# A mixture-of-experts layer computed slot by slot instead of with all experts for all rows

## The reference

```python
x = x + tanh(g_xattn[0]) * conv_attention(layernorm(x), ...)        # stage A
# stage B: 8 experts, 2 chosen for each row, and a shared expert
h = layernorm(x)
probs = softmax(h @ Wr)                     # [2048, 8]
weights, chosen = top_k(probs, 2)           # not renormalized
moe = sum over e of C[:, e] * ((silu(h @ Wg[e]) * (h @ Wu[e])) @ Wd[e])     # Wg, Wu: 256 x 176, Wd: 176 x 256
shared = sigmoid(h @ Wsg) * ((silu(h @ Sg) * (h @ Su)) @ Sd)                # 704 hidden columns
x = x + tanh(g_ffn[0]) * (moe + shared)
x = x + tanh(g_xattn[1]) * causal_attention(layernorm(x), ctx)      # stage C, 16 heads
x = x + tanh(g_ffn[1]) * lora_moe_ffn(layernorm(x))                 # stage D
```

## Time and profile before

| | us |
|---|---|
| runs before: median of 3 (lowest, highest) | 870.32 (870.18, 876.75) |
| the profiled execution | 869.0 |
| its span, first to last instruction | 867.3 |
| mean granted clock of TensorE | 0.96 of 2.4 GHz |

### The profile page before, as it was taken

The page is one execution under the profiler, slowest core; times in us unless marked ns, Lnnn a source line. Parts: engine busy times, 40 slices in busy tenths (PEclk is TensorE's granted clock), DMA queues, the critical chain, the costliest instruction groups (busy, mean ns, idle before and its releaser), DMA issues.

```text
span 867.3 us, 13423 instructions
## 1 busy us (share of the span) xinstructions
PE 781.8 (90%) x4612; PEld 634.5 (73%) x4627; DVE 566.6 (65%) x1022; ACT 314.5 (36%) x507; POOL 159.2 (18%) x211
## 2 busy tenths in 40 slices
PE   3887888799999999999997999976699999999994
PEld 2575766688888888888884555545588888888883
DVE  4877778454654574367546898983355876868764
ACT  2220211223423343342234878756143423324221
POOL 2977877300000000021100111111010000000000
PEclk9999999999999999999998999996599999999998
DMA  7221321000000000001001122200000000000000
GB/s 279 73 91 49 104 67 30 1 1 1 1 0 0 0 0 0 0 0 33 19 1 46 54 69 75 60 31 13 1 1 1 2 24 0 0 24 0 24 1 25
DMA packets 22134, 26.09 MB, mean 30 GB/s; under 512 B 5328, under 2 KB 17744, under 8 KB 21968
## 3 DMA queue, kind: packets, MB, share of 16 engines
q1 hardware_dynamic: 22096, 25.60, 9.3%
HBM read 23.22 MB, written 2.10 MB: 29 GB/s over the span
## 4 chain that ended last, share of the span: by engine, by line
PE 70%; DVE 15%; issue 6%; POOL 4%; ACT 2%; SPq 1%; DMA 1%; DVEq 0%; POOLq 0%; ACTq 0%
PE bank L1590 21%; PE bank L1457 19%; PE bank L1470 11%; PE bank L1522 3%; PE bank L1512 3%; POOL A L459 2%; DVE A L874 2%; PE bank L1532 1%; DVE small L1071 1%; PE bank L1599 1%; DVE A L863 1%; POOL R L450 1%; PE bank L1385 1%; PE bank L1504 1%; DVE A L1081 1%
## 5 line engine op out<-in xcount | busy, mean ns | idle before, releaser
L1590 PE MATMUL bank<-R 128*128 128x512 f32 (+3 forms) x1080 | 214.5, 359 | 11.2 <-DVE R L1235 4.9
L1590 PEld LDWEIGHTS bank<-R 128*128 128x128 f32 (+1 forms) x1080 | 181.0, 190 | 44.3 <-DVE R L1235 5.2
L1457 PE MATMUL bank<-R 128*128 128x512 f32 x768 | 186.2, 392 | 1.9 <-issue 1.9
L1457 PEld LDWEIGHTS bank<-R 128*128 128x128 f32 x768 | 140.3, 188 | 29.4 <-issue 2.1
L1019 DVE TENSOR_TENSOR A<-bank,A 128x512 f32<-128x512 f32 (+1 forms) x68 | 47.1, 692 | 114.0 <-PE bank L1457 111.7
L1470 PEld LDWEIGHTS bank<-R 128*128 128x128 f32 (+1 forms) x816 | 105.8, 190 | 10.5 <-issue 4.0
L1470 PE MATMUL bank<-R 128*128 128x256 f32 (+1 forms) x816 | 109.5, 284 | 2.5 <-DVE R L1029 2.2
L595 ACT ACTIVATE A<-bank 128x512 f32<-128x512 f32 (+1 forms) x68 | 40.7, 599 | 189.2 <-PE bank L1457 181.5
L874 DVE TENSOR_TENSOR A<-bank,A 128x512 f32<-128x512 f32 x64 | 43.8, 684 | 20.0 <-PE bank L1375 15.2
L1373 PE MATMUL bank<-A 128*128 128x256 f32 x128 | 40.9, 402 | 14.6 <-DVE A L874 13.6
L766 ACT ACTIVATE A<-bank 128x512 f32<-128x512 f32 (+1 forms) x48 | 28.6, 597 | 64.7 <-PE bank L1590 64.7
(11 more groups left out here) (163 smaller groups left out, 1038.9 us busy)
## 6 DMA issues: line engine op xcount, KB each, us to landing
A<-in_w SPq DMA_DIRECT2D x16, 384.0 KB, 3.1
A<-in_w SPq DMA_DIRECT2D x8, 480.0 KB, 3.6
A<-in_ctx_one SPq DMA_DIRECT2D x8, 272.0 KB, 3.6
A<-in_ctx_half SPq DMA_DIRECT2D x8, 256.0 KB, 3.1
A<-in_ctx_nat SPq DMA_DIRECT2D x4, 512.0 KB, 4.5
A<-in_ctx_t SPq DMA_DIRECT2D x128, 16.0 KB, 2.0
out<-X SPq DMA_DIRECT2D x4, 512.0 KB, 2.9
A<-in_filt SPq DMA_DIRECT2D x1, 1536.0 KB, 11.8
```

Of the source, the lines that this page charges most:

```text
L1457: mm = nc.tensor.matmul(dst[0:pr], wX[:, j, at + k * P:at + k * P + pr], mX[:, k], start=(n == 0), stop=(n == 5))
L1590: mm = nc.tensor.matmul(dst, a, m, start=start and n == 0, stop=stop and n == len(prods) - 1, skip_group_check=skip)
```

## The change

The experts' part of stage B is computed only for the rows that chose them. Each of the 4096 (row, choice) pairs gets a place in `xs`, a buffer in DRAM of NS = 39 slots of 128 rows, sorted by expert, each expert starting a new slot. The 39 slots are what 4096 pairs in 8 experts can need at most; their number is fixed, the expert of each slot is known at run time only.

- Stage B now runs `b_group(0..2)` (the 6 shared tiles alone, 512 rows at a time, in the order of groups 0, 3, 1, 2), then `e_slots`, then `b_group(3)`.
- TensorE counts the places (`b_positions`: 16 matmuls of 128 down to 8 columns and two more), VectorE makes addresses (`rank_step`, `place_step`, 16 steps each), POOL scatters the normed rows into `xs` by 32 indirect DMAs of 128 rows. SP has cleared `xs` with four DMAs of 1.2 to 1.3 MB in stage A.
- For each slot: SP loads 128 rows; TensorE turns them (2 transposes), ScalarE and VectorE split; 6 matmuls of 352 columns make gate and up with the rows on the partitions; Silu, product, 2 transposes, split; 6 matmuls of 256 columns; ScalarE copies the result to SBUF and issues the DMA that stores it in `ys`. TensorE reads the weights at addresses held in registers, which it fetches from SBUF for four slots at a time.
- POOL gathers the two results of each row by 32 indirect DMAs, and VectorE adds them to X, weighted (`mix_step`), groups 0 and 1 beside the last shared group, groups 2 and 3 in stage C. The norm statistics of stage C follow each group's mixing.
- The key buffer is cleared by VectorE in `b_group(3)`, no longer by POOL.
- Stage A: `a_bias` and `a_skip` are cut by batch, `a_sum` and `a_finish` of a group run at heads 3 to 5 of the next, with a second z2 buffer; the weights are split in halves (384 or 512 columns); the routing steps leave stage A, router turns and logits of two more groups come in. The loops of B and C over groups are unrolled.

The diff, cut to its core:

```diff
+NS = 2 * B + E - 1
+F2 = 2 * F0
+ORDER = (0, 3, 1, 2)
+XGS, YSS, GBS = 4, 4, 8
...
-TURN_A, BIAS_A, SKIP_A = 6, 8, 11
+TURN_A, BIAS_A, SKIP_A, ROOT_USED, SUM_A = 6, 7, 13, 12, 3
...
+            def load_slot(n):
+                if n >= XGS:
+                    sp.wait_ge(tx_done, n - XGS + 1)
+                sp.dma_start(xg[:, n % XGS], xs[n * P:(n + 1) * P]).then_inc(xg_loaded[n % XGS], 16)
+            sp.wait_ge(xs_written, 16 * 2 * B)
...
+            pool.wait_ge(where_ready, 1)
+            for i in range(G):
+                g = XN_ORDER[i]
+                pool.wait_ge(xn_ready, BG * (i + 1))
+                for t in range(BG * g, BG * (g + 1)):
+                    for r in range(2):
+                        q = r * B + t
+                        nc.gpsimd.indirect_dma_start(xs, bass.IndirectOffsetOnAxis(ap=where[:, q:q + 1], axis=0),
+                                                     XN[:, t], None).then_inc(xs_written, 16)
...
+            pool.wait_ge(edown_done, NS)
+            for u in range(YSS):
+                pool.wait_ge(ys_stored[u], 16 * len(range(u, NS, YSS)))
+            gather(0)
+            gather(1)
+            c_root(0)
+            gather(2)
+            c_root(1)
+            gather(3)
...
+            def e_take(n):
+                act.wait_ge(edown_done, n + 1)
+                if n >= YSS:
+                    act.wait_ge(ys_stored[n % YSS], 16 * (n // YSS))
+                nc.scalar.activation(yst[:, n % YSS], YP[n % 2][:, 0:D], ACT.Copy).then_inc(yst_ready, 1)
+                act.wait_ge(yst_ready, n + 1)
+                act.dma_start(ys[n * P:(n + 1) * P], yst[:, n % YSS]).then_inc(ys_stored[n % YSS], 16)
+            e_high_x(0)
+            for n in range(NS + 2):
+                if n + 1 < NS:
+                    e_high_x(n + 1)
+                if n < NS:
+                    e_silu_of(n)
+                if 1 <= n <= NS:
+                    e_high_h(n - 1)
+                if n >= 2:
+                    e_take(n - 2)
...
+            def mix_step(i, g):
+                t, r = BG * g + i // 2, i % 2
+                dve.wait_ge(y_gathered[t % GBS], 32 * (t // GBS + 1))
+                if r:
+                    dve.wait_ge(mixed, 2 * t + 1)
+                nc.vector.scalar_tensor_tensor(out=X[:, t], in0=gb[:, t % GBS, r], scalar=k12[:, r, t:t + 1],
+                                               in1=X[:, t], op0=ALU.mult, op1=ALU.add).then_inc(mixed, 1)
...
+            for n in range(NS + 1):
+                if n + 1 < NS:
+                    e_low_x(n + 1)
+                if n == 1:
+                    b_finish(2)
+                if n < NS:
+                    e_hidden(n)
+                if n:
+                    e_low_h(n - 1)
+            b_hidden(G - 1, 0)
+            b_group(G - 1, 0, [(1, Steps(clear_step, 16)), (1, mix_and_norm(0)), (1, mix_and_norm(1))])
+            b_finish(G - 1)
...
+            def e_ids(n):
+                m = min(4, NS - n)
+                for at, top in ((0, F2), (NS + 1, D)):
+                    _, vals = nc.values_load_multi_w_load_instructions(
+                        eid[:, at + n:at + n + m], engines=(mybir.EngineType.PE,), min_val=0, max_val=(E - 1) * top)
...
+            def e_gate_up(n, v):
+                pe.wait_ge(xsL_ready, n + 1)
+                if n >= 2:
+                    pe.wait_ge(eh_ready, n - 1)
+                m = 0
+                for xX, wX in ((xsH, wgH), (xsL, wgH), (xsH, wgL)):
+                    for k in range(DT):
+                        mm = nc.tensor.matmul(GU[n % 2][:, 0:F2], xX[:, n % 2, k * P:(k + 1) * P],
+                                              wX[:, bass.ds(v + k * E * F2, F2)], start=(m == 0), stop=(m == 5))
+                        m += 1
+                mm.then_inc(egu_done, 1)
...
+            def e_slots():
+                pe.wait_ge(eid_ready, 2)
+                for n in range(NS + 2):
+                    if n + 1 < NS:
+                        e_turn_x(n + 1)
+                    if n < NS:
+                        if n % 4 == 0:
+                            ids.append(e_ids(n))
+                        e_gate_up(n, ids[n // 4][0][n % 4])
+                    if n == NS:
+                        b_gate_up(G - 1, 0)
+                    if 1 <= n <= NS:
+                        e_turn_h(n - 1)
+                    if n >= 2:
+                        e_down(n - 2, ids[(n - 2) // 4][1][(n - 2) % 4])
...
-            with pe.Fori(0, G - 1) as g:
-                b_tiles(g, True)
-            b_tiles(G - 1, False)
+            for i in range(G - 1):
+                b_group(i)
+            e_slots()
+            b_group(G - 1)
+            c_first_q()
```

More of the change, by code:

```diff
@@ new lines, in mix_step, with mix_and_norm, one @@
+            def mix_step(i, g):
[5 more added lines that the diff above has]
+                                               in1=X[:, t], op0=ALU.mult, op1=ALU.add).then_inc(mixed, 1)
+            def mix_and_norm(g):
+                norm = c_norm(g)
+                def one(i):
+                    if i < 2 * BG:
+                        mix_step(i, g)
+                    else:
+                        if i == 2 * BG:
+                            dve.wait_ge(mixed, 2 * BG * (g + 1))
+                        norm.take(1)
+                return Steps(one, 2 * BG + norm.count)
@@ new lines, in b_group @@
+            def b_group(i, start, steps):
+                for j in range(1, SJ):
+                    beside = Steps()
+                    for begin, s in steps:
+                        if begin <= j and s.left():
+                            beside = s
+                            break
+                    b_hidden(i, j)
+                    beside.take(3)
+                    b_low(i, j - 1)
+                    beside.take(3)
+                if i < G - 1:
+                    b_low_x(i + 1)
+                b_low(i, SJ - 1)
+                for begin, s in steps:
+                    s.take_all()
@@ L1112, in c_steps @@
                     norm.take(4)
+                    if more and k == 1 and g < 2:
+                        norm = mix_and_norm(g + 2)
+                    if more and k == 7:
+                        norm.take_all()
                     if not more:
@@ L1324, in _ @@
+            c_shift(0, 2)
+            for g in range(G - 1):
                 c_steps(g, True)
-            step.leave(per, G - 1, start)
             c_steps(G - 1, False)
```

1077 lines of the change are left out of this document (655 added, 422 removed).

## The result

After: 879.43 us, median of 4 runs (878.27 to 881.27). Before, beside it: 872.66 (870.18 to 876.75). The ratio is 1.0103, 95% interval [1.0068, 1.0139]: 1% slower, where 841 was predicted. The profiled execution took 878.27 us, its span 876.4. First the page of after, then its table of busy time by stretch (columns: us, busy time of each engine with its instructions, granted clock, DMA share, GB/s); the stretches end at the first shared matmul, the first slot's first product, the last slot's last matmul, and C's first and last reduction.

A forecast was written before the change was run, and what follows sets the result against it. TensorE, busy for 90% of the span, was taken as the bound. B 31 less, A 8 less and C 10 more make -29: from 869.0 to 840, 841 as median. The forecast's own range was 822 to 863, the whole range 800 to 885.

The forecast's parts named there:

- three signs of being wrong: A slot over 4.15 us, an indirect DMA keeping POOL for 2 us, or C growing by more than 15.
- Term 2: B, scatter: 32 POOL DMAs at 1.2 us, mostly hidden behind the shared groups; 4 us stick out.
- Rival 3: POOL's indirect DMAs take 2.0 us each, so scatter and gathers end later: 886 us; chance 0.07.
- Term 1: B, shared groups 0 to 2 with turns, logits, counting and group borders on TensorE: 83 us.
- Term 3: B, 39 slots bound by TensorE: 3.4 us each, bounds 2.4 and 4.9; 138 us with filling and draining.
- rival 1: The slot runs at the bare array sum, starts hidden: 2.7 us a slot, 808 us; chance 0.22.
- Rival 2: TensorE's order, address arithmetic and lower clock bound the slot: 4.9 us a slot, 899 us; chance 0.13.
- Rival 4: ScalarE holds the slot because issuing the store blocks it 2.0 us: 4.0 a slot, 864 us; chance 0.08.
- Term 4: Last slot to C's first reduction: store landing, gathers, mixes and norms in a row, 44 us.
- Term 5: A: cut products and later head sums save 2 to 3 us a group, 8 us; bounds 0 and 18.
- Term 6: C: mixing and norms of groups 2 and 3 on VectorE add 10 us; bounds 0 to 15.
- D (0): Second feed-forward layer: stays as it is, 285 us before and predicted.

The follow-up runs named there:

- e2: The changed kernel with POOL's 32 scatters left out, so that the slots read zeros: 854.6 us, ratio 0.9817.
- e1: The changed kernel without the run-time bounds checks on the expert offsets, register loads kept: 846.0 us.
- e12: The e1 kernel with each slot's result stored by a DMA that SP issues in place of ScalarE: 842.8 us, ratio 0.9624.
- e16: The changed kernel without bounds checks, mixing and norm steps spread in C, A's second turn later, one small POOL addition behind each scatter and gather: 820.7 us, ratio 0.9434.
- e13: The e11 kernel with one small POOL addition behind each scatter in place of two: 832.9 us, ratio 0.9551.
- e15: The e11 kernel with the second turn of router rows two heads later in A's last group: 835.1 us, ratio 0.9591.
- e17: The e16 kernel with POOL's root for group 1's norm moved ahead of group 2's gathers: 826.9 us, ratio 0.9510.
- e11: The changed kernel without bounds checks, mixing and norm steps spread at 4 a tile in C, two small POOL additions behind each scatter: 835.4 us, ratio 0.9605.
- e4: The changed kernel with each of VectorE's 32 mixes cut to one column of 256: 866.2 us, ratio 0.9926.
- run 5: The changed kernel with two small POOL additions behind each of the 32 scatters: 867.9 us, ratio 0.9973.
- e10: The changed kernel without bounds checks and with mixing and norm steps spread at 4 a tile in C: 846.0 us.

## Why the prediction was wrong

It put the kernel at 841, with one chance in five for slower. One of its three signs of being wrong came true: C grew by more than 15. By its steps:

- **Term 2, the scatter (4 us predicted): the step that failed.** POOL's 1.2 us a DMA came true (1.265), by luck, as it was the middle of two far bounds; the first scatter was issued 52.6 us behind B's start for 45. The scatter was costed as time of POOL and of a transfer alone, hidden behind the shared groups, and what it does to the other engines was put at nothing, without a reason. It held them: 27.7 us between after and `e2`, some 21 of them the hold. Rival 3 gave 886 for DMAs of 2.0 us; its number is near, its mechanism didn't happen.
- **Term 1, the shared groups (83 us): 95 without scatters.** TensorE's work in them is 87 for the 79 that I had added up, and 8 of idle time lie at borders and around the counting; I had taken 4.
- **Term 3, the slots (3.4 us each): 2.98 on the mean, for two wrong reasons that offset each other.** The bare loop is 2.11, below my lower bound of 2.4: the transposes take 0.065 us each in a row for 0.13, and there are no starts (TensorE has no gap from slot to slot), as rival 1 had it. And the fetch of eight offsets, which I charged with 0.2 us a slot, 0.8 for four slots, took 2.28: the checks. Rival 2 had "its address must be formed in front of it" as the cause; it came as one block a fetch, for 27.4 us in all with the clock (`e1`). The bounds stand in the line that makes the load, and I didn't ask what executes them. My upper bound was loose too: 3.9 us for a slot at the half clock doesn't follow from the rows, which give 2.4 x 1.95 / 1.04 = 4.5. The 20 loads took 0.44 us on the mean, 0.33 the least. The Trainium skill (DMA: Bandwidth & Descriptors, latency and other measured facts) puts the floor at some 600 ns; this trace doesn't agree.
- **Rival 4, ScalarE holds the slot: refuted.** Issue 0.33 us, and `e12`, without that issue, gave the same 2.11.
- **Term 4, last slot to C (44): 47.9.** The reckoning held: where nobody is held (`e16`) it is 43.3, and in after the eight mixes of group 1 take 4.1 us for 4, its norm with the late root 7.4 for 5 + 3, the last additions 1.7 for 1.8. (The parts as I listed them add up to 45.3, not 44.) What I left out are the gathers' holds of ScalarE: two Silus 2.9 and 8.0 us late in after, 14.3 us in `e13`, 20.1 in `e15`. `e17` shows that the place of the root behind the gathers costs the head of C 4.9 us; whether they can be had stays open, as that run was held in C.
- **Term 5, A (-8): -0.3.** The cuts won 3.8 us up to the ninth head of the last group, with the sums of the group before done in both (VectorE's second product of that head, `a_z`, starts at 135.23 for 139.01, second and first row below), half of what I took. The rest of the last group gave it back; I had priced the turns moved into it at 3 us of TensorE's work, not at the wait that they bring (the last of the rows below), with the lower clock behind it. `e15` has the first shared matmul 6.0 us earlier than `e11`.

```profile
139.01 0.69 DVE L874 TENSOR_TENSOR A<-bank,A 128x512 f32<-128x512 f32 x1 [1.79 <-PE bank L1375]
135.23 0.69 DVE L1054 TENSOR_TENSOR A<-bank,A 128x512 f32<-128x512 f32 x1
144.06 1.97 PE L1720 MATMUL bank<-ident,A 128*128 128x128 f32 x8 [4.49 <-ACT A L707]
```

- **Term 6, C (+10): +19.3.** Some 9 are the mixes (`e4`), about what 16 x 0.5 us says. The other 10 no run takes apart; what else moved in are the norms' steps and roots, and the granted clock in C fell from 0.96 to 0.89 (0.96 stands in the first row below, 0.89 in the table of after). I had counted the norm that leaves C's head as a gain of C, but it stood ahead of the first reduction, outside it.
- **D (0): +3.7.** No instruction of it changed. The 32 matmuls of 8 columns near its head took 6.83 us for 3.73, at the lower of the two clock levels. The rows are C of before, then these matmuls before and after:

```profile
464.66:582.02 117.36, 107.60 (x954) 60.96 (x966) 102.51 (x167) 84.66 (x121) 16.83 (x9) 0.96 0.20 61
599.98 3.73 PE L1599 MATMUL bank<-gw_sb,A 128*128 128x8 f32 x32
605.36 6.83 PE L1979 MATMUL bank<-gw_sb,A 128*128 128x8 f32 x32
```

The misses add up: 8 (A), 35.6 and 3.9 less 21.8 (B), 9.3 (C), 3.7 (D) make 38.7; from the 838 that the steps give for the span it is 38 to 876.4. Without the miss in B's first part the kernel would have been faster, as forecast. That the others nearly cancel is luck: the slots' 21.8 hide as much elsewhere.

## What to carry to other kernels

Look at what an issuing engine does to the others, not only at how long it takes itself: DMAs that POOL issues one behind another cost engines that share nothing with them in the program. A pause of 0.14 us behind each scatter cured it here; behind the gathers the same pause did in one kernel (`e16`) and not in the next (`e17`), so look at the trace again. Where a register value carries bounds, the checks are instructions on the engine that uses it, here the critical one, and they are counted nowhere on the page: look at the records of its queue. Where a fix moves time and the total stays, look one stage on for the same cause (`e15`) before calling it worthless.

## What the hardware did that I had not expected

- With 32 indirect DMAs of POOL at 1.265 us apart the stretch to the first slot was 19 to 28 us longer than without them, some 6 of it their own length (an estimate, run 5). ScalarE was held in each of these profiles, together with VectorE or TensorE, from some 15 us behind the first DMA to some 5 us behind the last. At 1.40, 1.53 or 2.4 us apart they held nobody. Gathers at 1.34 us apart held nobody in `e16`; in `e17`, 16 in a row, VectorE came 7.5 us late and ScalarE 5.1, so a bound may lie near there. A quarter of the bytes changed nothing. The scatters of the back-to-back row still landed 2.2 us behind their issue, by the updates of their semaphore, up to the last, so the transfers themselves did not queue.
- Which engine is held beside ScalarE changes with small edits elsewhere in the programs. The time of one kernel without a pause varies (`e10`: 828.6 to 848.9 us); whether it is the hold that varies is not known, as only one execution has a profile. TensorE, when held, starts single matmuls at multiples of 0.70 us. What they all wait for stays open: no record names it. The Trainium skill (DMA: Bandwidth & Descriptors, latency and other measured facts) has the descriptors of such DMAs in rings in SBUF, fetched from there by all DMA engines, and suspects contention at those ports where it explains why two of the DMA engines are slower. It says so of DMA engines, not of ScalarE or TensorE. That the bytes don't matter fits, but no run here looked at a port.
- A pair of bounds check and assertion takes 0.28 us of TensorE's queue, and 78 such pairs, with the clock that their stops cost, make 27 us.
- VectorE's 0.17 us clamp took 2.18 beside POOL's subtraction of 2.21 in C (rows above) and ended with it, as if it had to wait for its end; no run tests this.
